# Keys' sine products one slot earlier, values' transposes four steps later, early rows sent in pairs

## What is computed

```
q, k, v = x @ Wq.T, x @ Wk.T, x @ Wv.T
q = q*cos + rotate_half(q)*sin         # the same for k
attn = softmax(causal(q @ k.T / sqrt(128)))
x1 = layernorm(x + (attn @ v) @ Wo.T)
weights, ids = top_k(softmax(x1 @ gate.T), 6)   # of 64 experts
out = layernorm(x1 + sum over chosen experts of silu(x1@g)*(x1@u)@d + shared expert)
```

## Time and profile before

| | us |
|---|---|
| three runs, median (lowest, highest) | 1418.35 (1413.24, 1418.37) |
| the profiled execution, its span | 1411.39, 1409.6 |
| TensorE busy, share of the span | 1264.9, 90% |
| VectorE busy | 1051.0, 75% |
| ScalarE busy | 854.4, 61% |
| GpSimd busy | 694.4, 49% |
| mean granted TensorE clock | 0.960 |

### The profile page before, as it was taken

One profiled execution on the slowest core, in us unless ns is written; L12 is line 12 of the kernel. 1 busy time (PEld: TensorE's weight loads), 2 busy tenths in 40 slices (PEclk: granted clock), 3 DMA queues, 4 the chain that ended last, 5 costly groups with the idle time before them and its releaser, 6 DMA issues. The chain is left out here.

```text
span 1409.6 us, 28399 instructions
## 1 busy us (share of the span) xinstructions
PE 1264.9 (90%) x8780; PEld 1125.1 (80%) x8780; DVE 1051.0 (75%) x2191; ACT 854.4 (61%) x1956; POOL 694.4 (49%) x718
## 2 busy tenths in 40 slices
PE   3899999999999999999989989972997999999965
PEld 2789789889889888978978878862665999999854
DVE  3778677777787768879877878846224999999956
ACT  2666566565566556566656656634114999999832
POOL 4433433433443443344464455413713888888830
PEclk8999999999999999999999999975998999999979
DMA  7676676675467775577576577612305888888868
GB/s 241 166 184 158 172 180 157 175 200 149 120 167 191 195 197 142 140 197 181 155 198 178 131 180 194 182 59 44 107 30 156 271 271 274 269 271 268 258 203 264
DMA packets 204439, 256.48 MB, mean 182 GB/s; under 512 B 11130, under 2 KB 177694, under 8 KB 204340
## 3 DMA queue, kind: packets, MB, share of 16 engines
q1 hardware_dynamic: 193300, 229.92, 60.3%
q0 software_dynamic: 11040, 25.30, 5.5%
HBM read 90.42 MB, written 169.72 MB: 185 GB/s over the span
## 5 line engine op out<-in xcount | busy, mean ns | idle before, releaser
L764 DVE TENSOR_REDUCE neg_max<-scores 128x1 f32<-128x256 f32 (+7 forms) x256 | 193.0, 754 | 150.4 <-PE scores L880 148.5
L536 ACT ACTIVATE pt_hi<-pt 128x512 fp32r<-128x512 f32 (+3 forms) x384 | 174.7, 490 | 190.7 <-PE pt L889 189.0
L509 ACT ACTIVATE probs<-scores,neg_max 128x256 f32<-128x256 f32 (+7 forms) x256 | 190.2, 743 | 55.8 <-DVE neg_max L764 55.4
L469 POOL TENSOR_TENSOR turned<-turned,turn_sin 128x512 f32<-128x512 f32 x80 | 102.9, 1286 | 230.3 <-DVE turn_sin L708 230.3
L789 PE MATMUL o_ps<-pt_hi,v_hi 128*128 128x256 f32 (+1 forms) x640 | 193.6, 303 | 21.5 <-DVE o_lo L728 21.2
L720 DVE TENSOR_TENSOR pt_lo<-pt,pt_hi 128x512 fp32r<-128x512 f32 (+3 forms) x384 | 200.7, 551 | 13.5 <-ACT pt_hi L536 10.3
L790 PE MATMUL o_ps<-pt_lo,v_hi 128*128 128x256 f32 (+1 forms) x640 | 179.6, 281 | 0.0
L791 PE MATMUL o_ps<-pt_hi,v_lo 128*128 128x256 f32 (+1 forms) x640 | 179.3, 280 | 0.0
L466 POOL TENSOR_TENSOR turned<-taken,cos 128x512 f32<-128x512 f32 x80 | 104.1, 1301 | 144.9 <-ACT taken L519 144.7
L889 PE MATMUL pt<-ident,probs 128*128 128x128 f32 x1152 | 169.5, 274 | 5.7 <-DVE pt_lo L720 4.4
L1422 POOL DMA_INDIRECT results_dram<-y_sb,dest x134 | 148.6, 1109 | 33.7 <-issue 27.3
(11 more groups left out here) (250 smaller groups left out, 3668.9 us busy)
## 6 DMA issues: line engine op xcount, KB each, us to landing
rows_dram<-empty SPq DMA_DIRECT2D x64, 2096.2 KB
up_raw<-in_up SPq DMA_DIRECT2D x69, 368.0 KB
x_in<-rows_dram SPq DMA_DIRECT2D x68, 258.0 KB
parts<-results_dram SPq DMA_DIRECT2D x16, 768.0 KB, 9.8
down_raw<-in_down SPq DMA_DIRECT2D x69, 128.0 KB
down_raw<-in_down_tail SPq DMA_DIRECT2D x69, 112.0 KB
w_raw<-in_w SPq DMA_DIRECT2D x8, 768.0 KB, 16.5
wo_raw<-in_wo SPq DMA_DIRECT2D x8, 512.0 KB, 19.4
```

Of the source, the lines that this page charges most:

```text
L509: nc.scalar.activation(probs[:, at_probs(k, m), 0:w], scores_ps[m % 2][:, score_cols(m)], ACT.Exp, bias=neg_max[:, m % 4:m % 4 + 1], accum ...
L536: nc.scalar.activation(pt_hi[m // 2 % 2][:, a:z, P * (m % 2):P * (m % 2) + P], pt_ps[c % 2][:, 0:P * (z - a)].rearrange("p (k q) -> p k q" ...
L764: nc.vector.tensor_reduce(neg_max[:, n % 4:n % 4 + 1], scores_ps[n % 2][:, score_cols(n)], AX.X, ALU.max, negate=True).then_inc(max_made, 1)
```

## The change

Three edits of the attention block. The sine of the keys is issued right after the step's maximum and for fill n-1, so one step number earlier and behind another instruction. Values move from 11 to 15 mod 16. The tables of the early routing are drawn anew, since turns, logits and places need steps without a fill; the sends go in two neighbouring steps of every four, and 28 steps of the last round are named by a rule.

```diff
-         "V": [16 * i - 5 for i in range(2 * KV_ROUND)],
+         "V": [16 * i - 1 for i in range(2 * KV_ROUND)],
...
-             (2, 19): [(1, "moments", 0), (1, "moments", 1)], (2, 21): [(0, "top", 0)], (2, 22): [(0, "top", 1)],
+             (2, 19): [(1, "moments", 0), (1, "moments", 1)], (2, 21): [(1, "inverse", 0)], (2, 22): [(1, "norm", 0)],
...
-EARLY_EXP = {(2, 32): 0, (3, 28): 1}
-EARLY_TURN = {(2, 3): (0, 0), (2, 15): (0, 1), (2, 63): (1, 0), (3, 3): (1, 1)}
-EARLY_LOGITS = {(2, 19): 0, (3, 15): 1}
-EARLY_PLACE = {(2, 31): 0, (3, 31): 1}
+EARLY_EXP = {(2, 48): 0, (3, 26): 1}
+EARLY_TURN = {(2, 3): (0, 0), (2, 11): (0, 1), (2, 27): (1, 0), (2, 35): (1, 1)}
+EARLY_LOGITS = {(2, 19): 0, (3, 3): 1}
+EARLY_PLACE = {(2, 51): 0, (3, 27): 1}
 RING_ROWS = 4
 SENDS = EARLY * WAYS
-EARLY_FILL = {step: f for f, step in enumerate([2 * STEPS + 49 + 2 * f for f in range(SENDS // 2)]
-                                               + [3 * STEPS + 41 + 2 * f for f in range(GT)]
-                                               + [3 * STEPS + 48 + f for f in range(SENDS // 2 - GT)])}
+EARLY_FILL = {step: f for f, step in enumerate([2 * STEPS + 54 + 4 * (f // 2) + f % 2 for f in range(SENDS // 2)]
+                                               + [3 * STEPS + n for n in range(41, 69) if n > 55 or n % 4 != 1])}
...
-                    if turn and turn[0] == "K" and runs(turn[1], per("K"), first, last):
-                        turn_by_sine(k, *turn)
                     if runs(n, STEPS, first, last):
 
                         dve.wait_ge(scored, now(k, STEPS, n + 1))
                         nc.vector.tensor_reduce(neg_max[:, n % 4:n % 4 + 1], scores_ps[n % 2][:, score_cols(n)],
                                                 AX.X, ALU.max, negate=True).then_inc(max_made, 1)
+                    if use and use[0] == "K" and runs(use[1], per("K"), first, last):
+                        turn_by_sine(k, *use)
```

More of the change, by code:

```diff
@@ L100 @@
              (2, 11): [(1, "stats", 1)], (2, 15): [(1, "stats", 2)], (2, 18): [(1, "stats", 3)],
-             (2, 19): [(1, "moments", 0), (1, "moments", 1)], (2, 21): [(0, "top", 0)], (2, 22): [(0, "top", 1)],
-             (2, 23): [(0, "ids", 0), (0, "ids", 1)], (2, 25): [(0, "mask", 0)], (2, 26): [(0, "mask", 1)],
-             (2, 27): [(0, "mask", 2), (0, "mask", 3)], (2, 29): [(0, "mask", 4)], (2, 30): [(0, "mask", 5)],
-             (2, 31): [(0, "shift", 0), (1, "inverse", 0)], (2, 35): [(0, "weigh", 0)], (2, 39): [(0, "weigh", 1)],
@@ L105 @@
[L105 to L114, removed]
@@ L115 @@
-             (3, 54): [(1, "slot", 8)], (3, 55): [(1, "slot", 9), (1, "slot", 10)], (3, 57): [(1, "slot", 11)]}
+             (2, 19): [(1, "moments", 0), (1, "moments", 1)], (2, 21): [(1, "inverse", 0)], (2, 22): [(1, "norm", 0)],
+             (2, 23): [(1, "norm", 1), (1, "norm", 2)], (2, 25): [(1, "norm", 3)], (2, 26): [(0, "top", 0)],
+             (2, 27): [(0, "top", 1), (0, "ids", 0)], (2, 29): [(0, "ids", 1)], (2, 30): [(0, "mask", 0)],
+             (2, 31): [(0, "mask", 1), (0, "mask", 2)], (2, 35): [(0, "mask", 3)], (2, 39): [(0, "mask", 4)],
@@ new lines @@
+             (2, 43): [(0, "mask", 5)], (2, 47): [(0, "shift", 0)], (2, 50): [(0, "weigh", 0)],
+             (2, 51): [(0, "weigh", 1)], (2, 53): [(0, "slot", 0)], (2, 54): [(0, "slot", 1)],
+             (2, 55): [(0, "slot", 2), (0, "slot", 3)], (2, 57): [(0, "slot", 4)], (2, 58): [(0, "slot", 5)],
+             (2, 59): [(0, "slot", 6), (0, "slot", 7)], (2, 61): [(0, "slot", 8)], (2, 62): [(0, "slot", 9)],
+             (2, 63): [(0, "slot", 10), (0, "slot", 11)], (3, 7): [(1, "top", 0)], (3, 11): [(1, "top", 1)],
@@ new lines @@
+             (3, 15): [(1, "ids", 0)], (3, 18): [(1, "ids", 1)], (3, 19): [(1, "mask", 0), (1, "mask", 1)],
+             (3, 21): [(1, "mask", 2)], (3, 22): [(1, "mask", 3)], (3, 23): [(1, "mask", 4), (1, "mask", 5)],
+             (3, 25): [(1, "shift", 0)], (3, 27): [(1, "weigh", 0), (1, "weigh", 1)], (3, 29): [(1, "slot", 0)],
+             (3, 30): [(1, "slot", 1)], (3, 31): [(1, "slot", 2), (1, "slot", 3)], (3, 35): [(1, "slot", 4)],
+             (3, 39): [(1, "slot", 5)], (3, 43): [(1, "slot", 6)], (3, 47): [(1, "slot", 7)],
@@ L116 @@
+             (3, 50): [(1, "slot", 8)], (3, 51): [(1, "slot", 9), (1, "slot", 10)], (3, 53): [(1, "slot", 11)]}
 EARLY_DEVIATION = {(1, 60): 0, (2, 20): 1}
-EARLY_EXP = {(2, 32): 0, (3, 28): 1}
-EARLY_TURN = {(2, 3): (0, 0), (2, 15): (0, 1), (2, 63): (1, 0), (3, 3): (1, 1)}
-EARLY_LOGITS = {(2, 19): 0, (3, 15): 1}
-EARLY_PLACE = {(2, 31): 0, (3, 31): 1}
+EARLY_EXP = {(2, 48): 0, (3, 26): 1}
+EARLY_TURN = {(2, 3): (0, 0), (2, 11): (0, 1), (2, 27): (1, 0), (2, 35): (1, 1)}
+EARLY_LOGITS = {(2, 19): 0, (3, 3): 1}
```

## The result

| | before | after |
|---|---|---|
| runs, median (lowest, highest), us | 1417.39 (1413.24, 1418.37) | 1440.80 (1440.35, 1442.58) |
| ratio, 95% interval | | 1.0173 (1.0150 to 1.0196) |
| profiled execution, its span, us | 1411.39, 1409.6 | 1440.53, 1438.8 |
| first step of the attention block | 30.13 | 32.13 |
| first normalization of the next block | 934.30 | 964.88 |

The change makes the kernel 1.7% slower: 23.4 us by the medians, 29 by the two profiled executions (that of before, 1411.39, was faster than any of the four behind its median). All of it lies in the attention block, whose successor starts 30.6 us later; from there to the end the kernel after is 1.4 us shorter (473.92 for 475.30 us).

A forecast was written before the change was run, and what follows sets the result against it. TensorE was taken as the bound, VectorE in steps 8 to 10 of small halves. Terms 11.5 + 4.9 - 2 - 4.3 + 3 = +13 us; forecast 1430, own range 1425 to 1435, 8-in-10 range 1408 to 1442.

The forecast's parts named there:

- What bounds the kernel: Attention block: TensorE is the bound, but VectorE bounds steps 8 to 10 of small halves, with 1.80 us idle behind `o_lo`.
- The sine in small halves: Keys' sine beside GpSimd's products takes 3.3 us, TensorE waits 3.2 us in fill 9; +1.55 us each, +11.5 over eight.
- In large halves: Keys' sine beside GpSimd's products delays `pt_lo` and TensorE's transposes: +0.7 us in each of 7 halves, +4.9.
- The values: Value transposes four steps later: `v_lo` waits shrink in small halves, arise in large ones; together -2 us, between -6 and +2.
- Early tables: Early routing spread anew over rounds 2 and 3: group 0 gives -2 us, turns and logits -1.4.
- Sends: Paired sends free steps of ScalarE's ring-slot wait, -1.4 us; 13 sends instead of 12 behind the last queries, +0.5.
- Clock: TensorE's granted clock after longer gaps in small halves: one or two falls more, +3 us, between -5 and +9.
- Rival (a): Sine's new place: no lock to speak of, or turns favouring VectorE; about -14 us, 1404, chance 0.18.
- (b): Lock at the sine's new place, but GpSimd's earlier addition gives time back, no more clock falls; +2 to +5, 1422, chance 0.26.
- (c): Clock falls in all 8 small halves and new tables hit full steps; +20 us, 1438, chance 0.08.

## Why the prediction was right, and where it was not

**What bounds the kernel:** right, and shown: taking the sine out of VectorE's steps 8 to 10 takes 1.6 us of wait out of step 10, and 1.1 net out of the small half.

**The sine in small halves:** right step by step. The sine was to take 3.3 us and takes 3.31; the sums were to end 5.14 us behind the start of step 8's maximum and end 5.06 behind it; the wait was to be 3.2 and is 3.02, and `o_ps` no longer waits. In (3,9) the wait is 2.08, as a send between the two products softens the lock. So the wait is 1.22 us longer than the 1.80 that it replaces; the prediction's +1.55 is 0.13 more than its own times give (273.81 + 1.71 - 274.10 = 1.42). What the sum lacked is that TensorE works its 1.71 us behind the wait at half the clock, 2.71 us. I had put all of that in one term of its own.

**In large halves:** +0.7 forecast, 0.65 measured.

**The values:** 0.93 us behind `v_lo` in small halves (1.1 forecast) and 0.40 in large ones (0.5). Rounds 0 and 1 gain nothing in sum. The term of -2 missed the start: with values at 15 and both the sine and the last sends at their old places the first step begins 2.0 us later (32.15 for 30.13), with the sine alone it doesn't (30.12). The size is not firm: one kernel with values at 15 began at 31.15.

**Early tables:** -3.4 forecast. Round 2 without sine and sends is 0.6 us shorter and round 3 equal, so about zero. Waits changed their names: `x_raw` 2.09 went, `pt_lo` 1.62 came.

**Sends:** the step that failed. I wrote that pairs "leave more steps free of ScalarE's wait for a ring slot" and took -1.4, and +0.5 for the end. Measured +12, between 7.5 and 12 by the several ways to count. I counted steps, where the queue decides: for a step with n mod 4 = 2 the send stands behind an addition that waits for a sine that VectorE makes in the step after. The row that says so was there before: GpSimd waited up to 5.2 us for `turn_sin` ahead of such an addition, and here with two sends right behind it.

```profile
876.11 1.30 POOL L469 TENSOR_TENSOR turned<-turned,turn_sin 128x512 f32<-128x512 f32 x1 [5.03 <-DVE turn_sin L708]
877.56 1.01 POOL L445 DMA_INDIRECT rows_dram<-early_rows,early_slots_int  x1
```

**Clock:** +3 forecast. It can't be added up by kernel, but by half it is +1.0 us in each of three small halves of rounds 0 and 1 and about 5 in that of (3,34), 8 at least. The price of 1.8 us for a step of 0.04 was near: with the same instructions and the same idle time the half of (0,34) took 44.14 us at 1.00 and 45.74 at 0.96 (the two kernels with the sine at its old place). The number of falls was too small, and the count that it started from was wrong: not 3 but 5 of the 8 small halves were below 1.00 before (0.93 in the first, 0.97 in that of (2,2)), and 7 of 8 are after.

Sine and clock together were forecast at 19.4 us and measured at 17.3 (the clock that the sends brought down is in their 12); the rest was forecast at -6.3 and came out at +13.3, of which the sends are 12.0 for -0.9 and values and tables 1.3 for -5.4. So the direction and its mechanism were right and the size was not. The sum was +13 us and the two profiled executions are 29 apart; 1430 was 12 us above the median shown, and the medians are 23.4 apart. 1440.8 lies outside the forecast's own range of 1425 to 1435, and only 1.2 us inside the wide one of 1408 to 1442. Rival (a), no lock, is excluded by the stretched rows, (b) by a wait that nothing gives back. (c) came nearest to the time, 1438, with a chance of 0.08, and named "new tables hit full steps" as one of its causes. Its first cause, clock falls in nearly all small halves, is there; the second was the ring and not the tables.

## What to carry to other kernels

The sine product of VectorE, with two operands in SBUF, took 0.69 us alone and 1.37 to 1.66 beside GpSimd's products in the rows shown: before moving such an instruction, look up which GpSimd instruction runs at the new place, and let the one that can wait do so. For a send or a copy that shares a queue with waiting work, count the time at which the queue reaches it, not the step at which it is listed. And put work without a near reader behind the operation that TensorE waits for next: a saved us of wait was worth about two here (2.6 us for 1.1, and 2.1 for 1.0), where the clock went up with it.

## What was not expected of the hardware

The Trainium skill, page "SBUF — State Buffer", section "Who interferes with whom", has the shared port held for a whole instruction. The trace agrees, and shows the order of the turns: in all the rows above the engine that had waited came next, so that two products of VectorE and one of GpSimd alternate and all three are stretched. An indirect send between GpSimd's two products did not take a turn: at (3,9), where one ran from 741.22 to 742.50, the second sine (from 741.62) took 0.68 us.

No wait alone sets the clock. The same instructions with the same wait of 3.02 us in (0,41) went on at half the clock in the kernel after (the matmul behind it took 0.58 us) and at the full one with the old steps of the last sends (0.39 us). In the kernel after the small halves of rounds 0 and 1 have a wait of 3.02 us and 0.93 (all four), but the first of round 2 has 3.04 us and 1.00; with the sine alone it was 3.0 us and 0.96. A wait of 2.0 us behind `v_lo` went with 1.00 in two halves and 0.96 in one, in both runs of that kernel. What else decides was not settled.

An indirect send took 10.3 us from issue to landing in the half of (3,34) of the kernel after (median of 7), beside the zero rows, for 9.0 in the same half before (median of 4). The lateness of the first send and this time are both in ScalarE's wait; what part the second has was not tried.
